# A fused adaLN / attention / FFN / GRU block: the first attention in groups of four heads over row quarters

## The reference

```python
x = x + attn0(cond0(x, c))        # first attention, then a second one with fp8 rounding
x = x + ffn0(resample(x, c))      # 2:4 sparse SwiGLU
x = x + attn1(gru(c, x))          # a GRU over 256 steps, then causal attention
x = x + ffn1(cond1(x))            # top-k tokens through a GELU FFN
```

```python
scale, shift = split(c @ W_emb + b_emb)
xn = rms_norm(x, g_norm) * (1 + scale) + shift
q, k, v = heads(xn @ W_qkv)                    # 16 heads of 16
q = rms_norm(q, g_q); k = rms_norm(k, g_k)     # per head
attn = softmax(q @ k.T * 16 ** -0.5)
o = attn @ v
y = o + o @ W_out                              # result of the first attention
qkv2 = y @ W_qkv2                              # start of the second
scale_of_fp8 = max(abs(.)) over all of q, of k and of v, all batches
```

## Time and profile before

| what | us |
| --- | --- |
| median of 3 runs | 1182.24 (1180.54 to 1185.33) |
| the profiled execution | 1184.23 |
| its span | 1182.4 |
| PE / PEld busy | 925.6 / 611.8 |
| DVE / ACT / POOL busy | 776.6 / 532.7 / 324.6 |
| first attention of the four batches, about | 53 to 257 |

### The profile page before, as it was taken

One profiled execution on the slowest core, in us unless ns is written; L12 is line 12 of the kernel. 1 busy time (PEld: TensorE's weight loads), 2 busy tenths in 40 slices (PEclk: granted clock), 3 DMA queues, 4 the chain that ended last, 5 costly groups with the idle time before them and its releaser, 6 DMA issues.

```text
span 1182.4 us, 40966 instructions
## 1 busy us (share of the span) xinstructions
PE 925.6 (78%) x16406; PEld 611.8 (52%) x16406; DVE 776.6 (66%) x2511; ACT 532.7 (45%) x2127; POOL 324.6 (27%) x431
## 2 busy tenths in 40 slices
PE   2699999957888856869696969696766599999726
PEld 2466665733444534546464545464544366677515
DVE  5766665757666556757666666666666667677574
ACT  2444453424444314646465656565555544354111
POOL 0740000002222043937465665757011000000000
PEclk9899999987998977989899999999999999999868
DMA  8000000020000000000000000000020000000101
GB/s 263 15 1 1 0 0 0 0 86 12 0 0 0 19 2 9 7 9 5 13 4 13 4 13 4 13 4 13 4 75 4 4 1 1 0 0 0 36 0 36
DMA packets 32539, 19.83 MB, mean 17 GB/s; under 512 B 23168, under 2 KB 29312, under 8 KB 32384
## 3 DMA queue, kind: packets, MB, share of 16 engines
q1 hardware_dynamic: 27200, 17.05, 4.9%
q10 hardware_dynamic: 5184, 0.59, 0.3%
HBM read 14.49 MB, written 1.05 MB: 13 GB/s over the span
## 4 chain that ended last, share of the span: by engine, by line
PE 50%; issue 20%; DVE 20%; ACT 4%; POOL 2%; DMA 1%; SPq 1%; ACTq 0%; POOLq 0%; DVEq 0%
PE banks L756 14%; PE banks L310 7%; PE banks L703 4%; PE banks L345 4%; DVE work L1044 3%; PE banks L726 3%; DVE h_ring L1058 3%; DVE gate_r L1040 3%; ACT nzh L890 3%; PE banks L1073 2%; PE banks L357 2%; DVE pre_n L1049 2%; PE banks L1459 2%; PE banks L283 1%; PE banks L492 1%
## 5 line engine op out<-in xcount | busy, mean ns | idle before, releaser
L756 PE MATMUL banks<-w_qkv,h_ring 128*4 128x64 f32 x12288 | 232.2, 225 | 116.7 <-DVE h_ring L1058 98.4
L756 PEld LDWEIGHTS banks<-w_qkv,h_ring 128*4 128x4 f32 x12288 | 181.5, 90 | 220.8 <-DVE h_ring L1058 198.2
L310 PE MATMUL banks<-shared,qT 128*128 128x256 f32 (+2 forms) x640 | 156.8, 353 | 7.7 <-DVE nraw L438 3.3
L283 PE MATMUL banks<-zero 128*128 128x512 bf16 x413 | 129.1, 397 | 10.1 <-DVEq L1645 4.2
L414 ACT ACTIVATE probs_b<-banks,nraw 128x256 f32<-128x256 f32 (+1 forms) x256 | 99.8, 444 | 77.1 <-DVE nraw L438 44.2
L881 ACT ACTIVATE banks<-gate_r 128x8 f32<-128x8 f32 x256 | 46.3, 181 | 182.7 <-DVE gate_r L1040 181.9
L1040 DVE STREAM_TRANSPOSE gate_r<-banks 128x64 f32<-128x64 f32 x256 | 64.0, 250 | 79.5 <-PE banks L756 75.7
L310 PEld LDWEIGHTS banks<-shared,qT 128*128 128x128 f32 (+1 forms) x640 | 96.0, 175 | 30.5 <-DVE nraw L438 12.1
L438 DVE TENSOR_REDUCE nraw<-banks 128x2 f32<-128x512 f32 x128 | 85.1, 687 | 13.6 <-PE banks L310 12.7
L1044 DVE STREAM_TRANSPOSE work<-banks 128x64 f32<-128x64 f32 x256 | 76.6, 299 | 5.1 <-PE banks L756 4.8
L448 DVE COPY work<-banks 128x512 f32<-128x512 f32 (+1 forms) x104 | 64.2, 617 | 19.9 <-PE banks L357 16.8
(11 more groups left out here) (304 smaller groups left out, 1685.4 us busy)
## 6 DMA issues: line engine op xcount, KB each, us to landing
big<-in_x SPq DMA_DIRECT2D x1, 1024.0 KB, 6.1
w_gate<-in_L_ffn_w_gate SPq DMA_DIRECT2D x1, 1024.0 KB, 11.0
shared<-in_L_ffn_w_down SPq DMA_DIRECT2D x1, 1024.0 KB, 5.7
w_gate<-in_L_ffn_W SPq DMA_DIRECT2D x1, 1024.0 KB, 6.5
shared<-in_L_ffn_W SPq DMA_DIRECT2D x1, 1024.0 KB, 6.7
out_x<-big SPq DMA_DIRECT2D x4, 256.0 KB, 2.2
w_qkv<-in_L_cond_W_qkv SPq DMA_DIRECT2D x1, 768.0 KB, 7.4
w_qkv<-in_L_attn_W_qkv SPq DMA_DIRECT2D x1, 768.0 KB, 9.1
```

Of the source, the lines that this page charges most:

```text
L283: nc.tensor.matmul(bank[:, :], zero16[:, 0:P], zero16[:, :], start=True, stop=True, skip_group_check=True)
L310: mm = nc.tensor.matmul(out, qT[:, c, tile], k[:, c, 0:n], start=True, stop=not causal, skip_group_check=True)
L756: mm = nc.tensor.matmul(bank[32 * j:32 * j + B, 0:64], h_col(t, c), w_hh[:, c, g, :].rearrange("p (m n) -> p m n", m=KC)[:, :, 32 * j:32 * ...
```

## The change

Phase 1 is written anew; the other phases keep their work.

- **Groups of four heads.** `kz` is not used in phase 1. A group of four heads has its queries and keys in the four row quarters (32 partitions each) of `qTs` and `kTs`; `scores` multiplies quarter by quarter with a contraction of 32, head j into bank j, for both halves of the queries: 8 matmuls of 256 columns. One reduce takes the 2 x 4 maxima from the four banks and writes them, negated, into the padding column of the queries in `qkps`. `rows_again` turns these 128 columns once more, VectorE copies them to `qRs`, and `by_key` computes the scores once more with keys as rows and queries as columns; the keys' padding column holds 1.0, so that the maximum is inside the product. One exponential of 2048 elements follows, and its result is already turned the way `values` wants it. The turning of the probabilities and its copies are gone.
- **Batches interleaved.** No loop: the four batches are written out, with two sets of tiles. Projection, turning and normalisation of the next batch and the output work of the one before are put between the steps of the groups. `w_gate` serves as the second `qkps`, so its load moves behind phase 1.
- **Norm.** Squares, inverse root (one power of 128x64) and the product with it move to GpSimd; the product of g_q, g_k and 16 ** -0.5 is one column `g_col`, applied to the queries when they are copied from PSUM. Its values are loaded by 8 small DMAs instead of two broadcasts. GpSimd's copy to `aT` is gone.
- **Weights fused.** W2 + W W2 (W is W_out, W2 is W_qkv2) is computed once by `fused_weights`, so the output projection of each batch and the addition are gone.
- Semaphores of later phases are merged and renumbered; their work is the same.

```diff
+            def scores(b, g):
+                G = 4 * b + g
+                if G:
+                    pe.wait_ge(a_exp, G)
...
+                for t in range(ST):
+                    for j in range(4):
+                        r = slice(32 * j, 32 * j + 32)
+                        mm = nc.tensor.matmul(bank[j][:, t * S:(t + 1) * S], qTs[b % 2][r, g, t * P:(t + 1) * P], kTs[b % 2][r, g, :],
+                                              start=True, stop=True, skip_group_check=True)
+                mm.then_inc(a_s, 1)
...
+            for b in range(B):
+                scores(b, 0)
+                if b:
+                    out_rows(b - 1, 0)
+                heads_in(b, 0, 1)
+                rows_again(b, 0)
+                if b:
+                    values(4 * b - 1)
+                by_key(b, 0)
+                if b:
+                    out_rows(b - 1, 1)
+                heads_in(b, 1, 1)
...
+                scores(b, 1)
+                if b:
+                    out_cols(b - 1)
+                if b + 1 < B:
+                    qk_in(b + 1, 0)
+                rows_again(b, 1)
+                values(4 * b)
+                by_key(b, 1)
+                if b + 1 < B:
+                    qk_in(b + 1, 1)
...
+                scores(b, 2)
+                if b + 1 < B:
+                    v_in(b + 1)
...
+                rows_again(b, 2)
+                values(4 * b + 1)
+                by_key(b, 2)
+                if b:
+                    second_qk(b - 1, 0)
...
+                scores(b, 3)
+                if b:
+                    second_qk(b - 1, 1)
+                    second_v(b - 1)
...
+                rows_again(b, 3)
+                values(4 * b + 2)
+                by_key(b, 3)
+                if b + 1 < B:
+                    for side in range(2):
+                        heads_in(b + 1, side, 0)
...
+                    act.wait_ge(a_k, 4 * b + g + 1)
+                    nc.scalar.activation(quads[g % 2], quad_s, ACT.Exp).then_inc(a_exp, 1)
...
+            def normalised(b):
+                for t in range(ST):
+                    pool.wait_ge(a_qkvc, 3 * b + t + 1)
+                    nc.gpsimd.tensor_tensor(sq[:, t, :], tmp[:, t, :], tmp[:, t, :], ALU.mult).then_inc(a_sq, 1)
+                pool.wait_ge(a_ms, b + 1)
+                ch.done(nc.gpsimd.tensor_tensor(rq[:, :, :], nrm[:, :, :], half[:, :].rearrange("p (t h) -> p t h", t=ST), ALU.pow))
+                if b >= 2:
+                    pool.wait_ge(a_r, 4 * b - 4)
+                ch.done(nc.gpsimd.memset(qkps[b % 2][:, :, 0:NH, HD], 0.0))
+                for t in range(ST):
+                    nc.gpsimd.tensor_tensor(qkps[b % 2][:, t, :, 0:HD], tmp[:, t, :].rearrange("p (h e) -> p h e", e=HD), bcast_heads(rq[:, t, :]), ALU.mult).then_inc(a_qkn, 1)
...
+                    v.wait_ge(a_s, G + 1)
+                    nc.vector.tensor_reduce(qkps[b % 2][:, :, 4 * g:4 * g + 4, HD].rearrange("p t h -> p h t"),
+                                            quad_s.rearrange("p (j t k) -> p j t k", j=4, t=ST), AX.X, ALU.max, negate=True).then_inc(a_max, 1)
+                    v.wait_ge(a_r, G + 1)
+                    nc.vector.tensor_scalar(qRs[G % 2], pR[:, 0:S], g_col[:, 0:1], None, ALU.mult).then_inc(a_re, 1)
...
-            with pe.Fori(0, B) as i:
-                keep_warm(6, pT[0])
-                pe.wait_ge(rd_act, i + 1)
-                head_rows(pe, i)
-                pe.wait_ge(s_vcp, i + 1)
-                attn_pe(pe, 0, i, ahead=lambda t: project(i + 2, t))
-                out_proj(pe, i, 0, w_out1)
```

More of the change, by code:

```diff
@@ L180, in build @@
         narrow = (qkp16, qT16, kz16, lambda b: b.bitcast(BF16)[:, 0:512])
+        qkps = [qkp, w_gate[:, :, :].rearrange("p c n -> p (c n)").rearrange("p (t h e) -> p t h e", t=ST, e=32)]
+        vs = [v_sb, work[:, 2048:3072].rearrange("p (t h e) -> p t h e", t=ST, e=VW)]
+        kTs = [shared[:, 1024 * n:1024 * (n + 1)].rearrange("p (g s) -> p g s", g=HC) for n in range(2)]
+        qTs = [qT, shared[:, 2048:3072].rearrange("p (g s) -> p g s", g=HC)]
+        qRs = [shared[:, 3072 + S * n:3072 + S * (n + 1)] for n in range(2)]
+        quads = [work[:, 3072:5120], probs_b[:, :, :].rearrange("p a b -> p (a b)")]
+        quad_s = banks8[:, 0:2048]
+        pR, pX, pY = pM
         zero8 = sb("zero8", [P, ST, 4])
@@ L225, in build @@
         s_am, s_gmax, s_v8 = sem("s_am"), sem("s_gmax"), sem("s_v8")
[L226 to L227 removed]
+        (e_grid, e_gm, e_xg, e_xgc, e_gate, e_up, e_gc, e_uc, e_hid, e_kept0, e_kept1, e_tr, e_trc, e_dn, e_x2, p_step, gm_step) = (sem("e_" + n) for n in (
+            "grid gm xg xgc gate up gc uc hid kept0 kept1 tr trc dn x2 pstep gmstep").split())
         e_kept = (e_kept0, e_kept1)
@@ L234, in build, with from_pe @@
             "h hist rm nm zm tr tn tz sr sz th pn zh gi ni gd nd act g2 sdr sdn sdz open row0").split())
[L236 to L240, removed]
+        (f_wtc, f_x3c, f_ks, f_kms, f_kr, f_score, f_sh, f_aexp, f_att, f_attd, f_projc, f_yT, f_var, f_rs8, f_dg, f_lx, f_sel, f_fxc, f_selTc, f_wsh, f_wexp, f_tw, f_gelu, f_xw, f_out,
+         f_pe) = (sem("f_" + n) for n in (
+            "wtc x3c ks kms kr score sh aexp att attd projc yT var rs8 dg lx sel fxc selTc wsh wexp tw gelu xw out pe").split())
+        in_order = (("wt", 2), ("x3", 4), ("keys", 1), ("srow", 1), ("attb", 1), ("proj", 1), ("y", 4), ("lb", 1), ("wrow", 1), ("fx", 1), ("selT", 1),
+                    ("h1", 2), ("twc", 1), ("ol", 1), ("sc", 4))
+        before = {n: sum(c for _, c in in_order[:k]) for k, (n, _) in enumerate(in_order)}
+        def from_pe(name, n):
+            return before[name] + n
         brT = sb("brT", [P, KC, B * NBLK])
@@ new lines, in phase1_pool, with resampling @@
+        def phase1_pool(pool):
+            ch = Chain(pool, gm_step)
+            def normalised(b):
+                for t in range(ST):
+                    pool.wait_ge(a_qkvc, 3 * b + t + 1)
+                    nc.gpsimd.tensor_tensor(sq[:, t, :], tmp[:, t, :], tmp[:, t, :], ALU.mult).then_inc(a_sq, 1)
+                pool.wait_ge(a_ms, b + 1)
+                ch.done(nc.gpsimd.tensor_tensor(rq[:, :, :], nrm[:, :, :], half[:, :].rearrange("p (t h) -> p t h", t=ST), ALU.pow))
+                if b >= 2:
+                    pool.wait_ge(a_r, 4 * b - 4)
+                ch.done(nc.gpsimd.memset(qkps[b % 2][:, :, 0:NH, HD], 0.0))
+                for t in range(ST):
+                    nc.gpsimd.tensor_tensor(qkps[b % 2][:, t, :, 0:HD], tmp[:, t, :].rearrange("p (h e) -> p h e", e=HD), bcast_heads(rq[:, t, :]), ALU.mult).then_inc(a_qkn, 1)
+            def resampling(b):
+                for dst, idx, w in ((gmats[b], x0, wt0), (gm1, ix1, wt1)):
+                    for k in range(KC):
+                        a = nc.gpsimd.tensor_scalar(dst[:, k, :], idx[:, b, :], cst[:, C_PART + k:C_PART + k + 1], None, ALU.is_equal)
+                    ch.done(a)
+                    for k in range(KC):
+                        a = nc.gpsimd.tensor_tensor(dst[:, k, :], dst[:, k, :], w[:, b, :], ALU.mult)
+                    ch.done(a)
+                nc.gpsimd.tensor_tensor(gmats[b], gmats[b], gm1, ALU.add).then_inc(e_gm, 1)
+                pool.wait_ge(e_gm, b + 1)
+            normalised(0)
+            pool.wait_ge(e_grid, 1)
+            for b in range(B):
+                resampling(b)
+                if b + 1 < B:
+                    normalised(b + 1)
+            pool.wait_ge(a_qkn, 2 * B)
+            pool.sem_inc(rd_pool, 4)
+            phase2_pool(pool)
@@ L1084, in phase5_pe @@
                 pe.wait_ge(rd_dve, i + 14)
[L1085 to L1089, removed]
+                head_rows(pe, i + 4, extra=4)
+                pe.wait_ge(s_vcp, i + 1)
+                attn_pe(pe, 4, i, causal=True, ahead=lambda t: project(i + 2, t))
+                out_proj(pe, i, 4, w_out3)
+                end_round(pe, s_proj, i + 5, rd_pe)
             phase6_pe(pe)
@@ L1404, in _ @@
             next_round(sp, 5)
+            sp.dma_start(w_gate[:, :, :], rows(d["L0_ffn_w_gate"])).then_inc(ld_ud, 16)
             sp.dma_start(w_down, rows(d["L0_ffn_w_down"])).then_inc(ld_ud, 16)
@@ L1503, in _ @@
             next_round(act, 1)
[L1505 to L1531 removed]
+            phase1_act(act)
         @block.gpsimd
@@ L1540, in _ @@
             next_round(pool, 1)
[L1541 to L1559 removed]
+            phase1_pool(pool)
         @block.vector
@@ L1629, in _ @@
             next_round(v, 1)
[L1630 to L1648 removed]
+            phase1_dve(v, chain.n)
 _INS = [
```

512 lines of the change are left out of this document (342 added, 170 removed).

## The result

The changed kernel takes 1147.2 us (median of 4 runs, 1137.25 to 1149.61) against 1182.87 us for the kernel before in the same comparison: a ratio of 0.970, 95% interval 0.966 to 0.975. That is 35.7 us less. Forecast were 1136 (46.4 less) and a range of 1112 to 1162. The direction and the range held; about a quarter of the forecast gain is missing.

A forecast was written before the change was run, and what follows sets the result against it. TensorE bounded the kernel before; afterwards the serial chain of a group would. First scores 54.1, batches 35.35 + 2 x 35.9 + 46.6, plus 3 for the clock, end at 210.8 instead of 257.16: 1136 us, range 1112 to 1162.

The forecast's parts named there:

- power of 128x64: Inverse roots as one power on GpSimd, growing by element: 9.9 us, making GpSimd late at the borders between batches.
- first scores: Start of the first attention's scores, behind input, power, products and heads: at 54.1 us against 53.99 before.
- row-quarter block, warm: Scores of four heads in four row quarters at once, 16 passes of 256 columns: 1.07 us.
- warm group: Serial chain of one group of four heads, from scores through maximum and scores by key to exponential: 7.9 us.
- extra of group 3: Transposes of group 3 wait behind both second projections and ScalarE's emptying of pR: 1.9 us more.
- start of group 2 to next scores: Stretch of a batch through GpSimd's squares, power and products until the next batch's heads are ready: 20.1 us.
- batches 0, 1, 2: Lengths of the first three attention batches, with GpSimd late at their ends: 35.35, 35.9 and 35.9 us.
- last batch: Batch 3, with nothing to interleave at its end, so output steps run in series: 46.6 us.
- half clock, all: Allowance for TensorE's slower clock after idling at the borders and in the beginning: 3 us in all.
- Rival B: Weight loads do not overlap in row-quarter blocks: 1.85 us a block, 1154 us in total; chance 0.14.
- rival C: Row quarters run one after the other: 3.64 us a block, 1210 us in total; chance 0.09 together with half clock.
- Rival A: GpSimd's power is cheap, a fixed 1.64 us, so the stalls go: 18 us less, 1118 in total; chance 0.15.

The follow-up runs named there:

- best version: Changed kernel with power by tiles, more products of zeros, batch 0's inverse root on ScalarE and VectorE, second V projection of batches 0 to 2 in another PSUM bank: 1119.26 us.
- root of batch 0 elsewhere: Changed kernel with power by tiles, more products of zeros, and batch 0's inverse root by ScalarE's square root, VectorE's reciprocal and one Newton step: 1122.65 us.

## Why the prediction was right or wrong

| step | forecast | measured |
|---|---|---|
| input ready | 29.95 | 29.22 |
| power of 128x64 | 9.9 | 10.56 |
| first scores | 54.1 | 53.33 |
| row-quarter block, warm | 1.07 | 1.15 |
| maximum, query copy, exponential | 2.3, 0.42, 1.9 | 2.29, 0.48, 1.88 |
| warm group | 7.9 | 8.07 to 8.32 |
| extra of group 3 | 1.9 | 1.72 to 1.97 |
| start of group 2 to next scores | 20.1 | 21.2, 20.9, 20.9 |
| batches 0, 1, 2 | 35.35, 35.9, 35.9 | 39.5, 39.7, 40.3 |
| last batch | 46.6 | 49.75 |
| half clock, all | 3 | about 11 (worked out below) |
| end | 210.8 | 222.65 |

**What bounds it.** Right. TensorE's 48 us of work a batch gave way to the chain of one group, and its pieces were priced within 0.1 us each. The chain alone was forecast at 33.9 us a batch; freed of waits it is 34.6, the difference being 0.17 to 0.2 a group.

**The row quarters.** Right: 1.15, nearest to all four at once. Rival B (1.85) is excluded by that row, rival C by it and by the run on one quarter, whose 3.72 a block is C's 3.64. C's time was too kind, though: the run is at 1314, not near 1210, and the clock fell as well (22 blocks at half clock are alone some 76 us). The Trainium skill (TensorE: Matmul & The Clock Gate, Measured speedup vs the span model) gives a ratio of 3.07 for four row quarters of 512 columns. The rows here, with 256 columns, give 3.72 / 1.15 = 3.2, and the estimate of 1.30 a block that the prediction worked out from that ratio lies above the 1.15 measured.

**The power.** Right that it grows by element and that it makes GpSimd late: 128x32 takes 5.43 and 128x64 10.57, 0.16 us for each further element, against the 0.147 from two small sizes. It cost 0.66 more than forecast at each of the places where it is on the chain, and with handovers the stretch was 0.8 to 1.1 longer at three borders, 2.7 us in all. Rival A was only an "if", but its price was about right: 20 us by the medians, 24 by the ends of the traces, for 18. In part that is luck, since its 18 held only 3 for the half clock.

**The half clock: the step that failed.** This is a term of the sum that was sized too small, 3 us where about 11 were lost. The forecast had TensorE idle 4 us at each border and added 3 us in all. The trace has waits of 4.27, 2.31 and 2.31, and behind each of them the first scores take 2.09; behind the first two, values and scores by key (in part or wholly) are at half clock too, and single cold groups (9.64 and 9.58 between exponentials) stand in batches 0 and 3. Taken apart at unchanged waits, the borders gave back 3.1, 3.3 and 0.95 us, and 10.8 us were gained in the medians. I had priced the heads behind a wait (0.9) and, but for the 3 us, not the steps of the chain behind the heads, though the earlier trace rows show a 4.2 us wait and the earlier trace rows a clock of 0.51 in the stage after it.

**The sum.** From first scores to the start of group 2 the batches were forecast at 15.25, 15.8 and 15.8 us and took 18.3, 18.85 and 19.5; that is 9.8, of which about 1.2 is the slower warm group (in the best version, all at full clock, the same stretches take 15.8, 16.1 and 16.1) and 8.6 the half clock. The stretch through GpSimd adds 2.7. The last batch adds 3.1, of which some 2.4 are two cold groups (0.94 before its first exponential, 1.5 before its second). So the half clock is 8.6 + 2.4, about 11. The first scores give back 0.8, and 3 were allowed for: 9.8 + 2.7 + 3.1 - 0.8 - 3 = 11.8, which is 222.65 - 210.8.

**Rest.** The later phases kept their length, as assumed, but it varies from execution to execution by several us (915 to 931 over the runs of this study), so totals agree less well than ends. Two small slips of the prediction don't change its sum much: its own rows give 31.05 - 0.94 = 30.11 for the input, not 29.95, and batch 0 lacks only the 1.9 us of extras in group 3, not 2.1, since its group 2 takes 8.32 like the others.

## What to carry to other kernels

When a slow step on a side engine makes TensorE wait, price the wait and also the chain behind it at half clock: at the three borders here the waits were 8.9 us and the half clock behind them 7.4. Cut such a step into pieces that can start with their inputs before looking for work to put in its shadow. Time freed ahead of a later bound is given back in full: first remove the wait, then shorten what stands before it.

## What the runs showed of the hardware

- GpSimd's power in f32 took 1.64 us for 128x8, 5.43 for 128x32 and 10.57 for 128x64, so 0.16 us for each further element of a partition; the product of the same 128x64 took 0.32. ScalarE's square root of the same tile took 0.26 and two table loads of 1.28 each, and VectorE's four steps behind it 1.22 (root of batch 0 elsewhere).
- The order in which row quarters are issued made hardly a difference (1.15 and 1.17 us a block), though one order changes quarter with every product and the other only after both halves.
- The busy share doesn't tell the clock: with all score products in one row quarter TensorE was 97% busy in one stretch and was granted 0.60, where the kernel before at 92 to 94% was granted 0.99 to 1.00. The cause is open.
- After a wait of 2.31 us, 1.09 of transposes at full clock and another 1.10 idle, the scores ran at half clock, at both later borders of the changed kernel.
